# Gated cross-attention with FFN on one core: the weights product taken from the loaded Wq with its correction as a 257th column, and the lead's chains split over ACT, DVE and GpSimd

## The reference

```
xn  = layernorm(x);  Q = xn @ Wq.T + bq;  K = ctx @ Wk.T + bk
S   = Q K^T, masked keys at -inf;  A = softmax(S)
x1  = x + tanh(g_xattn) * ((A @ ctx) @ Wo.T + bo)
W   = +1 where weights >= 0, else -1
out = x1 + tanh(g_ffn) * clip((layernorm(x1) @ W.T) * scale + bias, -100, 100)
```

## Time and profile before

| | us |
|---|---|
| median of three runs | 78.45 |
| lowest and highest of them | 78.12, 79.25 |
| the profiled execution's own time | 78.7 |
| its span, first to last instruction | 76.9 |

### The profile page before, as it was taken

One profiled execution on the slowest core, in us unless ns is written; L12 is line 12 of the kernel. 1 busy time (PEld: TensorE's weight loads), 2 busy tenths in 40 slices (PEclk: granted clock), 3 DMA queues, 4 the chain that ended last, 5 costly groups with the idle time before them and its releaser, 6 DMA issues.

```text
span 76.9 us, 1578 instructions
## 1 busy us (share of the span) xinstructions
PE 70.6 (92%) x528; PEld 65.7 (85%) x528; DVE 56.4 (73%) x164; ACT 37.2 (48%) x100; POOL 52.8 (69%) x98
## 2 busy tenths in 40 slices
PE   2999899998999999999999999999999989899920
PEld 2997797997999899989998999999899979778500
DVE  2492995699669489929984996679489656899940
ACT  0421527495695529444941775095529444703030
POOL 6005648899707408989999998899999999824300
PEclk9999999999999999999999999999999999999999
DMA  1899997998100000040003000400040040030025
GB/s 12 274 363 349 353 337 201 363 361 282 48 4 0 0 0 0 0 137 12 0 4 136 0 0 0 136 9 0 0 136 0 9 136 1 0 136 0 0 79 194
DMA packets 8139, 7.83 MB, mean 102 GB/s; under 512 B 836, under 2 KB 7876, under 8 KB 8132
## 3 DMA queue, kind: packets, MB, share of 16 engines
q1 hardware_dynamic: 7664, 7.60, 30.2%
q10 hardware_dynamic: 468, 0.14, 0.8%
HBM read 5.64 MB, written 2.10 MB: 101 GB/s over the span
## 4 chain that ended last, share of the span: by engine, by line
PE 81%; DVE 6%; ACT 6%; issue 2%; POOL 1%; POOLq 0%
PE ps_Z L579 14%; PE ps_K L579 12%; PE ps_S L642 10%; PE ps_F L579 8%; PE ps_O L661 8%; PE ps_x1T L687 5%; PE ps_cT L574 4%; PE ps_xT L574 4%; PE ps_x1T L574 3%; PE ps_K L693 2%; DVE w_cent L525 2%; PE ps_S L650 2%; DVE cT_lo L399 2%; ACT K_sb L225 2%; PE ps_x1T L751 1%
## 5 line engine op out<-in xcount | busy, mean ns | idle before, releaser
L424 DVE SCALAR_TENSOR_TENSOR x_sb<-ps_O,recip_p,xb_sb 128x256 f32<-128x256 f32 x14 | 6.1, 480 | 7.3 <-PE ps_O L661 7.3
L335 POOL TENSOR_TENSOR xb_sb<-x_sb,bo_g 128x256 f32<-128x256 f32 x16 | 11.4, 739 | 0.0
L341 POOL TENSOR_TENSOR f_biased<-f_scaled,bi_g 128x256 f32<-128x256 f32 x12 | 8.6, 738 | 3.1 <-DVE f_scaled L434 3.1
L210 ACT CAST cT_hi<-ps_cT 128x512 fp32r<-128x512 f32 x8 | 4.7, 586 | 12.5 <-PE ps_cT L574 12.5
L323 POOL TENSOR_SCALAR xn<-x_sb,rstd_x,off_x 128x256 f32<-128x256 f32 x16 | 10.0, 631 | 0.5
L579 PE MATMUL ps_Z<-woT_hi,cT_hi 128*128 128x256 f32 x32 | 9.7, 304 | 0.0
L642 PEld LDWEIGHTS ps_S<-K_sb,xT 128*128 128x128 f32 x64 | 7.8, 192 | 1.5 <-issue 0.8
L579 PE MATMUL ps_Z<-woT_lo,cT_hi 128*128 128x256 f32 x32 | 9.0, 280 | 0.0
L579 PE MATMUL ps_Z<-woT_hi,cT_lo 128*128 128x256 f32 x32 | 9.0, 280 | 0.0
L579 PE MATMUL ps_K<-cT_hi,wqk_hi 128*128 128x256 f32 x30 | 8.5, 283 | 0.5 <-DVE wqk_lo L404 0.5
L642 PE MATMUL ps_S<-K_sb,xT 128*128 128x128 f32 x64 | 8.6, 277 | 0.4 <-ACT K_sb L225 0.2
(11 more groups left out here) (145 smaller groups left out, 210.8 us busy)
## 6 DMA issues: line engine op xcount, KB each, us to landing
x_sb<-in_x_dram SPq DMA_DIRECT2D x8, 256.0 KB, 6.5
ctx_sb<-in_ctx_dram SPq DMA_DIRECT2D x8, 256.0 KB, 7.5
out_dram<-out_sb SPq DMA_DIRECT2D x7, 256.0 KB, 2.1
wq_sb<-in_L_xattn_Wq_dram SPq DMA_DIRECT2D x1, 256.0 KB, 2.9
wk_sb<-in_L_xattn_Wk_dram SPq DMA_DIRECT2D x1, 256.0 KB, 3.2
wo_sb<-in_L_xattn_Wo_dram SPq DMA_DIRECT2D x1, 256.0 KB, 4.8
w_sb<-in_L_ffn_weights_dram SPq DMA_DIRECT2D x1, 256.0 KB, 5.7
bo_all<-in_L_xattn_bo_dram SPq DMA_DIRECT2D x1, 128.0 KB, 5.6
```

The source lines that it names most:

```text
L335: nc.gpsimd.tensor_tensor(xb_sb[:, r], x_sb[:, r], bo_g[:], ALU.add).then_inc(xb_done, 1)
L341: nc.gpsimd.tensor_tensor(f_biased[:, r], f_scaled[:, r], bi_g[:], ALU.add).then_inc(f_biased_done, 1)
L424: nc.vector.scalar_tensor_tensor(out=x1_sb[:, r], in0=ps_O[:, b], scalar=recip_p[:, r:r + 1], in1=xb_sb[:, r], op0=ALU.mult, op1=ALU.add). ...
```

## The change

It has seven parts.

- The weights product uses `wq_sb`, as loaded. The row number (mean and bq) is written into a new column 256 of `wq_sb`; the product then has a 257th column, which holds for each of its rows the number to be added (`wqk_add`). ACT adds it to the first half as the bias of the conversion to `wqk_hi`; DVE converts the second half. `split_wqk` adds it too. The two halves of the product stand one behind the other, ahead of the ctx transposes.
- `wq2` is still needed for `kbias`; GpSimd makes it.
- The warm-up is 9 fp32 matmuls of a zero tile `blank`, written by DVE, and no longer 18 transposes of `ident`.
- bq and bk are loaded on SyncE's queue, behind Wq and behind ctx of group 0, instead of ACT's. The load of Wq into rows of 257 elements is a transfer of two runs of 256 per partition.
- For group 0 ACT copies xT before it waits for K's second half; the gate matmul and tanh come ahead of K of group 0.
- The first half of `xn` of group 0 is made by ACT.
- On DVE `mask_blk` moves behind the statistics of group 1, and `w_sum` and `w_mean` come ahead of `woT_lo`.

```diff
-WARM_UP = 18
+WARM_UP = 9
...
-            sp.dma_start(wq_sb[:], wq.rearrange("(p c) d -> p c d", c=DC)).then_inc(wq_loaded, 16)
+            sp.dma_start(wq_sb[:, :, 0:D], wq.rearrange("(p c) d -> p c d", c=DC)).then_inc(wq_loaded, 16)
+            sp.dma_start(bq_col[:], bq.rearrange("(p c) -> p c", c=DC)).then_inc(bq_loaded, 16)
             sp.dma_start(wk_sb[:], wk.rearrange("(p c) d -> p c d", c=DC)).then_inc(wk_loaded, 16)
             load_x(0)
             load_ctx(0)
+            sp.dma_start(bk_col[:], bk.rearrange("(p c) -> p c", c=DC)).then_inc(bk_loaded, 16)
...
             def evict_K(g):
                 act.wait_ge(kbias_ready, 1)
                 for c in range(DC):
+                    if g == 0 and c == 1:
+                        evict_xT(0)
                     if g == 0 and c == 0:
                         act.wait_ge(K0_half_prod, 1)
                     else:
                         act.wait_ge(K_prod, g + 1)
-                    if g == 0 and c == 1:
-                        evict_xT(0)
...
-            for c in range(DC):
-                act.wait_ge(ps_wqk_ready, c + 1)
-                nc.scalar.copy(wqk_hi[:, c], ps_wqk[c]).then_inc(wqk_hi_ready, 1)
-                if c == 0:
-                    evict_cT_hi(0)
+            act.wait_ge(ps_wqk_ready, 1)
+            nc.scalar.copy(wqk_add[:, 0:1], ps_wqk[0][:, D:D + 1]).then_inc(wqk_add_done[0], 1)
+            act.wait_ge(wqk_add_done[0], 1)
+            nc.scalar.activation(wqk_hi[:, 0], ps_wqk[0][:, 0:D], ACT.Identity, bias=wqk_add[:, 0:1]).then_inc(wqk_hi_ready, 1)
+            evict_cT_hi(0)
+
+            act.wait_ge(off_x_done, 1)
+            nc.scalar.activation(xn[:, 0, 0], x_sb[:, 0], ACT.Identity, scale=rstd_x[:, 0:1], bias=off_x[:, 0:1]
+                                 ).then_inc(xn_first_done, 1)
             act.wait_ge(ps_kbias_ready, 1)
             nc.scalar.copy(kbias[:], s_bank[:, 0:DC]).then_inc(kbias_ready, 1)
-            evict_K(0)
             act.wait_ge(ps_gate_ready, 1)
             nc.scalar.activation(tanh_g[:], o_bank[:, 0:2], ACT.Tanh).then_inc(tanh_ready, 1)
+            evict_K(0)
...
+            pool.wait_ge(wq_add_done, 1)
+            for c in range(DC):
+                nc.gpsimd.tensor_scalar(wq2[:, c], wq_sb[:, c, 0:D], wq_sb[:, c, D:D + 1], None, ALU.add).then_inc(wq2_ready, 1)
...
+            nc.vector.memset(blank[:], 0.0).then_inc(blank_ready, 1)
...
-            nc.vector.scalar_tensor_tensor(out=wq_add[:], in0=wq_sum[:], scalar=-1.0 / D, in1=bq_d[:], op0=ALU.mult,
+            nc.vector.scalar_tensor_tensor(out=wq_sb[:, :, D], in0=wq_sum[:], scalar=-1.0 / D, in1=bq_d[:], op0=ALU.mult,
                                            op1=ALU.add).then_inc(wq_add_done, 1)
-            dve.wait_ge(wq_add_done, 1)
-            for c in range(DC):
-                nc.vector.tensor_scalar(wq2[:, c], wq_sb[:, c], wq_add[:, c:c + 1], None, ALU.add).then_inc(wq2_ready, 1)
             stats_x(0)
             split_wqk(0)
+
+            dve.wait_ge(ps_wqk_ready, 2)
+            nc.vector.tensor_copy(wqk_add[:, 1:2], ps_wqk[1][:, D:D + 1]).then_inc(wqk_add_done[1], 1)
+            dve.wait_ge(wqk_add_done[1], 1)
+            nc.vector.tensor_scalar(wqk_hi[:, 1], ps_wqk[1][:, 0:D], wqk_add[:, 1:2], None, ALU.add).then_inc(wqk_hi_ready, 1)
+            split_wqk(1)
+            split_cT(0)
+            stats_x(1)
             dve.wait_ge(place_done, 1)
...
+            pe.wait_ge(blank_ready, 1)
+            for _ in range(WARM_UP):
+                nc.tensor.matmul(ps_x1T[:, 0, 0:P], blank[:], blank[:], start=True, stop=True)
             pe.wait_ge(ident_ready, 1)
             pe.wait_ge(consts_ready, 2)
-            for _ in range(WARM_UP):
-                nc.tensor.transpose(ps_x1T[:, 0, 0:P], ident[:], ident[:])
             pe.wait_ge(wk_loaded, 16)
+            pe.wait_ge(wq_add_done, 1)
             for m in range(DC):
-                for e in range(DC):
-                    if m == 0:
-                        pe.wait_ge(wq2_ready, e + 1)
-                    last = nc.tensor.matmul(ps_wqk[m], wk_sb[:, e, m * P:(m + 1) * P], wq2[:, e], start=(e == 0),
-                                            stop=(e == DC - 1))
-                last.then_inc(ps_wqk_ready, 1)
-                if m == 0:
-                    transpose_ctx(0)
+                accumulate(ps_wqk[m], [(wk_sb[:, e, m * P:(m + 1) * P], wq_sb[:, e]) for e in range(DC)]
+                           ).then_inc(ps_wqk_ready, 1)
+            transpose_ctx(0)
             pe.wait_ge(bk_loaded, 16)
+            pe.wait_ge(wq2_ready, DC)
```

More of the change, by code:

```diff
@@ L68, in gated_xattn_ffn @@
         ps_PT = s_bank[:, GB * P:2 * GB * P].rearrange("p (b q) -> p b q", b=GB)
-        ps_wqk = [k_bank[:, 0:D], z_bank[:, 0:D]]
+        ps_wqk = [k_bank[:, 0:D + 1], z_bank[:, 0:D + 1]]
         ps_woT, ps_w2T = by_chunk(f_bank), by_chunk(f_bank)
@@ L96, in gated_xattn_ffn @@
         x1T_hi, x1T_lo = sb("x1T_hi", [P, 2, DC, T], F32R), sb("x1T_lo", [P, 2, DC, T], F32R)
-        wq_sb, wk_sb, wq2 = sb("wq_sb", [P, DC, D]), sb("wk_sb", [P, DC, D]), sb("wq2", [P, DC, D])
+        wq_sb, wk_sb, wq2 = sb("wq_sb", [P, DC, D + 1]), sb("wk_sb", [P, DC, D]), sb("wq2", [P, DC, D])
         bq_col, bk_col = sb("bq_col", [P, DC]), sb("bk_col", [P, DC])
-        bq_d, wq_sum, wq_add = sb("bq_d", [P, DC]), sb("wq_sum", [P, DC]), sb("wq_add", [P, DC])
+        bq_d, wq_sum, wqk_add = sb("bq_d", [P, DC]), sb("wq_sum", [P, DC]), sb("wqk_add", [P, DC])
         wqk_hi, wqk_lo = sb("wqk_hi", [P, DC, D], F32R), sb("wqk_lo", [P, DC, D], F32R)
@@ L122, in gated_xattn_ffn @@
         sel = sb("sel", [P, G, P], BF16)
-        ones_1 = sb("ones_1", [1, P])
+        ones_1, blank = sb("ones_1", [1, P]), sb("blank", [P, P])
         x_loaded, ctx_loaded = [sem(f"x_loaded{g}") for g in range(G)], [sem(f"ctx_loaded{g}") for g in range(G)]
@@ L128, in gated_xattn_ffn @@
                              "bo_loaded", "sc_bi_loaded", "mask_loaded", "stored"))
+        xn_first_done = sem("xn_first_done")
+        blank_ready = sem("blank_ready")
         zeroed, ident_ready, consts_ready, mask_filled, place_done, group_of_done, sel_done, mask_ready = (
@@ L132, in gated_xattn_ffn @@
                              "sel_done", "mask_ready"))
+        wqk_add_done = [sem(f"wqk_add{c}_done") for c in range(DC)]
         bq_d_done, wq_sum_done, wq_add_done, wq2_ready, ps_wqk_ready, wqk_hi_ready, wqk_lo_ready = (
@@ L201, in _ @@
         def _(act):
-            act.dma_start(bq_col[:], bq.rearrange("(p c) -> p c", c=DC)).then_inc(bq_loaded, 16)
-            act.dma_start(bk_col[:], bk.rearrange("(p c) -> p c", c=DC)).then_inc(bk_loaded, 16)
             act.dma_start(mask_u8[:], mask).then_inc(mask_loaded, 16)
@@ L320, in norm_x @@
                     pool.wait_ge(xT_prod, g - 2)
-                for b in range(GB):
+                for b in range(1 if g == 0 else 0, GB):
                     r = g * GB + b
@@ L403, in split_wqk @@
                 dve.wait_ge(wqk_hi_ready, c + 1)
-                nc.vector.tensor_tensor(wqk_lo[:, c], ps_wqk[c], wqk_hi[:, c].bitcast(F32), ALU.subtract
-                                        ).then_inc(wqk_lo_ready, 1)
+                nc.vector.scalar_tensor_tensor(out=wqk_lo[:, c], in0=ps_wqk[c][:, 0:D], scalar=wqk_add[:, c:c + 1],
+                                               in1=wqk_hi[:, c].bitcast(F32), op0=ALU.add, op1=ALU.subtract
+                                               ).then_inc(wqk_lo_ready, 1)
             def split_x1T(g):
@@ L482, in _ @@
             dve.wait_ge(wq_loaded, 16)
-            nc.vector.tensor_reduce(wq_sum[:], wq_sb[:], AX.X, ALU.add).then_inc(wq_sum_done, 1)
+            nc.vector.tensor_reduce(wq_sum[:], wq_sb[:, :, 0:D], AX.X, ALU.add).then_inc(wq_sum_done, 1)
             dve.wait_ge(bq_loaded, 16)
@@ L500, in _ @@
                                         ).then_inc(mask_ready, 1)
-            split_cT(0)
-            split_wqk(1)
-            stats_x(1)
             stats_x(2)
@@ L507, in _ @@
             nc.vector.tensor_scalar(w_sign2[:], w_sb[:], 0.0, 2.0, ALU.is_ge, ALU.mult).then_inc(sign2_done, 1)
+            dve.wait_ge(sign2_done, 1)
+            nc.vector.tensor_reduce(w_sum[:], w_sign2[:], AX.X, ALU.add).then_inc(w_sum_done, 1)
+            dve.wait_ge(w_sum_done, 1)
+            nc.vector.tensor_scalar(w_mean[:], w_sum[:], 1.0 / D, None, ALU.mult).then_inc(w_mean_done, 1)
             dve.wait_ge(woT_hi_ready, 1)
@@ L518, in _ @@
                 if i == 0:
-                    dve.wait_ge(sign2_done, 1)
-                    nc.vector.tensor_reduce(w_sum[:], w_sign2[:], AX.X, ALU.add).then_inc(w_sum_done, 1)
-                    dve.wait_ge(w_sum_done, 1)
-                    nc.vector.tensor_scalar(w_mean[:], w_sum[:], 1.0 / D, None, ALU.mult).then_inc(w_mean_done, 1)
                     dve.wait_ge(w_mean_done, 1)
@@ L588, in transpose_x @@
             def transpose_x(g):
-                pe.wait_ge(xn_done, GB * (g + 1))
```

(5 more changed lines are left out.)

## The result

The changed kernel took 80.58 us in the median of four runs (80.11 to 81.38), the kernel before, timed beside it, 78.28: a ratio of 1.027, 95% interval 1.021 to 1.033. It is slower where 78.1 was forecast and 79.0 was the range's upper end. The profiled execution took 80.45 us with a span of 78.5, against 78.7 and 76.9.

The account below looks back on a forecast made before the run. TensorE is busy throughout 18.29 to 61.17 us, so the lead decides: 0.32 less Z's 0.02 saves 0.30, span 76.6, plus 1.8 gives 78.4; less the profiled run's 0.25 excess, 78.15, put at 78.1. Range (8 in 10): 77.0 to 79.0.

Parts of the forecast that it names:

- The start of the product: Lead: the weights product starts 0.5 us earlier, running from 5.1 to 6.73 where it ended at 7.23.
- the rival of the late load: SyncE's queue: bq lands at 5.46 behind Wq, the product starts at 6.05, time 79.0; chance 15%.
- The second half at full clock: Lead, TensorE: the second half of the weights product takes 0.82 us at the full clock.
- The warm-up's 0.46 us of earlier start: Lead, TensorE: waiting only for a DVE memset, the warm-up begins at about 0.95 instead of 1.50 and ends at 5.05.
- the sum: Whole kernel: 0.32 less Z's 0.02 is 0.30 us gained, span 76.9 to 76.6, forecast 78.1 us.
- Conversions: ACT and DVE behind the product: conversions get longer, 0.43 us back; K of group 0 at 9.71, 0.07 earlier.
- xT off the chain: ACT, group 0: xT's copy is hidden between K's halves, 0.57 us; scores start at about 12.38, 0.64 earlier.
- Z waits for DVE: Before Z of group 0: TensorE waits for `woT_lo`, 0.66 us lost; Z starts at 14.80 against 14.78.
- The wait for `w_cent`: Before attention of group 0: TensorE's wait for `w_cent` goes, 0.32 us gained.
- PT: Before attention of group 0: next late after `w_cent`; ACT ends it at 18.48, so attention can start at 18.62.
- `wq2` on GpSimd: Lead: two additions on GpSimd take 1.14, done by about 6.0, hidden by 2 us before the bias matmuls.
- The clock rival: Lead, TensorE: matmul warm-up raises the clock earlier, whole first product at 2.4 GHz, time 77.2; chance 17%.

Follow-up runs that it names:

- experiment 4: Kernel before with only the bq and bk loads moved to SyncE's queue, bq behind Wq, bk behind ctx of group 0: 79.10 us, ratio 1.009.
- experiment 1: Changed kernel with the bq and bk loads back on ACT's queue, nothing else: 78.44 us, ratio 1.000.
- experiment 5: Changed kernel timed again, no edit, in two sets on different chips: first set 79.19 us, ratio 1.008; second set 80.68 us.
- experiment 6: Changed kernel with 4 warm-up matmuls instead of 9: 81.02 us, ratio 1.031.
- experiment 3: Changed kernel with w_sum and w_mean put back behind the low part of ctx of group 1: 78.65 us, ratio 1.001.
- experiment 2: Changed kernel with 12 warm-up matmuls instead of 9: 79.18 us, ratio 1.011.
- experiment 8: Changed kernel with the old warm-up, 18 transposes of the identity: 79.21 us, ratio 1.010.
- experiment 11: Changed kernel with bq and bk loads back on ACT's queue and w_sum, w_mean back behind the low part of ctx of group 1: 77.86 us, ratio 0.994.
- experiment 7: Kernel before with the early xT copy and 6 warm-up transposes instead of 18: 80.01 us.
- experiment 9: Kernel before with only xT's copy ahead of the wait for K's second half, gate matmul and tanh ahead of K: 77.49 us, ratio 0.988.

## Why the prediction was wrong

**The start of the product: the failing step.** The prediction put Wk's landing at "at most 4.80" and the start at 5.1; they were 5.70 and 5.95. It took one slot of issue (0.44) and a landing 3.2 us behind it. The split load of Wq took 0.63 to issue and bq behind it 0.58, so Wk was issued at 2.04 and not 1.60, and it landed 3.65 later, since the transfers ran at 214 GB/s. Experiments 4 and 1 give most of this to the two bias loads in SyncE's queue: with them on ACT's, Wk landed at about 5.0 and the product started at 5.41. bq itself landed at 1.41 + 2.6 = 4.0, before the 4.26 forecast: the rival of the late load named the right queue and the wrong transfer. The small load was punctual; the large one behind it was not.

**The second half at full clock: the step that made it 80.6 and not 79.** The prediction took 0.82 us for it and looked only at a clock that rises earlier. In the result's profile it took 1.73. What matters is not the kind of warm-up but that it ended before the product could start: where the clock had not risen by the end of the standstill, it came only at 9.6 (result) or after 10.4 (experiments 5 and 6). The counts: 12 of the 30 runs with nine matmuls and Wk late (result, experiments 3 and 5) took 80.1 or more. Of the 29 runs of the changed product with a standstill of 0.53 us at most in the trace (experiments 1, 2, 8, 11) none did, nor did any of the 95 of the kernel before, of which 17 were timed beside experiment 5's second set. With the warm-up cut short all five runs of experiment 6 took 79.96 or more, and experiment 7 has it in the old order. That nine matmuls can be enough all the same, with a standstill as long as 1.49 us (experiment 3), these counts say as well. The warm-up's 0.46 us of earlier start, priced as a gain, was the standstill's cause together with Wk. The kernel before had no gap: its warm-up ended at 5.60 with `wq2` ready. Where the clock was up in time, the rest of the sum held: in experiment 5's first set K started 4.08 us behind the product's start (6.41, 10.49); the sum had 4.61 with a first half at half speed, which is 0.5 dearer. Those runs took 78.7 to 79.5, the price of the late start without the clock.

**Conversions.** Right by their sizes: 0.16 and 0.47 on ACT, 0.40 from one scalar-operand row to the next on DVE, 0.74 from the start of `cT_lo` to K for the 0.81 of the sum. `cT_lo` started 1.14 after the product's end, since that end, and not the first half's chain, was the bound.

**xT off the chain.** 0.46 us (2.78 against 3.24), forecast 0.57. Experiment 9 shows that it reaches the end of the kernel.

**Z waits for DVE.** As forecast: from `cT_lo`'s start to `woT_lo`'s 4.93 us, sum 5.02; from the scores to Z 2.21, sum 2.42. Moving `w_sum` back gave 0.5 us here, and 0.6 between experiments 1 and 11 by the medians, on two chips (0.3 by what each was below its kernel before).

**The wait for `w_cent`.** Gone, as forecast. From Z to attention 3.78 against 4.16, 0.38 for the 0.32 of the sum. PT was next late, as named.

**`wq2` on GpSimd** took 1.83 and not 1.14 and stayed hidden: done at 6.94, the bias matmuls came at 10.04.

**The clock rival.** It rested on matmuls counting where transposes do not, which the Trainium skill ("TensorE: Matmul & The Clock Gate", Part 4: PE-mode transpose) states. Experiment 8 goes the other way: 18 transposes of fp32, no matmul, and the first pass of the product at the upper level, 2.4 GHz. The measurement decides.

**The sum.** K 1.83 late = 0.35 (chain start of the product, 5.95 against 5.60) + 0.42 (first half, slower by 2.05 - 1.63 with the release from idle in it) + 1.73 + 1.14 + 0.74 (product's second half, to `cT_lo`, to K) - 2.55 (before: from the first half's end at 7.23 to K at 9.78) = 1.83. From there the two gains, 0.46 and 0.38, less 0.45 lost before Z, leave 1.44 at attention; the last ACT copy has 1.54, and 0.10 of that came in the loop and the tail.

What stays open is what decides between the outcomes in a single execution, with the same kernel and the same gap, why the executions of 80.1 us and more gather in some sets (4 of 4 and 5 of 6 against 1 and 2 of 10), and with that what the change costs on a given chip. Wk's order ahead of bq on SyncE's queue was not tried.

## What to carry to other kernels

A warm-up is there to hand TensorE over without a gap, with its clock up; before one starts it earlier or shortens it, find which load releases the first real product and make the warm-up outlast it. Against executions whose clock was up in time this gained nothing here (79.18 against 79.19); what it can take away is the others, of which there were none in the 29 runs without a long standstill. A tiny load placed ahead of a large one on the queue that the start waits for can cost far more than its bytes (here Wk landed 1.4 us later in experiment 4): read the landing of the one behind it. And when two parts of an edit act on the path's start, time the unchanged kernel again before a single experiment is believed: two outcomes 1.5 us apart looked here like the effect of two DVE rows, and of three more warm-up matmuls.
